# A two-layer sequence kernel on one core: the attention's numerator on GpSimd, and three reorderings of TensorE and VectorE work

## The reference

```python
x = L0_attn_hidden                                  # (2, 1024, 128)
x = layernorm(x + rwkv_attention(x))                # block 1: recurrence over time
x = layernorm(x + fp8_linear(x))                    # block 2
x = layernorm(x + conv_gate_long_convolution(x))    # block 3: by FFT in the reference
x = layernorm(x + routed_experts(x))                # block 4: 2 rounds, top 2 of 8 experts

# block 1, per time step (expo 0, 1 and 2 of the kernel are e1s, e2s and e2/e1):
out = (e1 * num + e2 * cv) / (e1 * den + e2)        # the attention's output
num, den = e1s * num + e2s * cv, e1s * den + e2s    # the state
rwkv = (sigmoid(r) * out) @ Wo

# block 4, twice:
shared_ctrl = gelu(ctx @ w_s1 + b_s1) @ w_s2 + b_s2
ctrl = gelu(ctx_e @ w1[expert] + b1) @ w2[expert] + b2
x_next, v_next = mix(inl(shared_ctrl, ...), inl(ctrl, ...))
halt = sigmoid(gelu(x_next @ w_h1 + b_h1) @ w_h2 + b_h2)
integrated += halt * (gelu(x_next @ w_f1 + b_f1) @ w_f2 + b_f2) * integration_weight
```

## Time and profile before

| | |
|---|---|
| median of 3 runs | 454.08 us (452.54 to 455.95) |
| the profiled execution's own time | 453.8 us |
| span of its instructions | 452.0 us |
| TensorE | 409.1 us busy, 91% of the span |
| VectorE | 337.3 us, 75% |
| ScalarE | 192.9 us, 43% |
| GpSimd | 21.8 us, 5% |
| the chain that ended last | TensorE 64%, VectorE 13%, ScalarE 3%, issue 2% |

### The profile page before, as it was taken

How to read it: one execution, slowest core, us unless ns; L and a number is a source line. 1 busy time by engine, 2 the same in 40 slices (tenths; PEclk the granted TensorE clock), 3 DMA queues, 4 the chain that set the end, 5 groups by cost and what they waited for, 6 DMA issues and landing times.

```text
span 452.0 us, 4385 instructions
## 1 busy us (share of the span) xinstructions
PE 409.1 (91%) x1494; PEld 215.4 (48%) x1494; DVE 337.3 (75%) x688; ACT 192.9 (43%) x318; POOL 21.8 (5%) x38
## 2 busy tenths in 40 slices
PE   4791987979999999999999889999999999999992
PEld 1341565667976375354544343433644433443361
DVE  5999998977882996879988994697654862374565
ACT  1342669452226513445255355344055626225431
POOL 1000203021000000000000000000000000000001
PEclk9896999879999999999999989999999999999997
DMA  6300000040000000000000000000000000000001
GB/s 227 133 1 0 1 1 0 2 151 0 1 1 0 1 1 0 0 1 1 1 1 0 0 1 23 0 1 1 0 0 1 24 1 0 1 0 0 0 1 46
DMA packets 4886, 7.10 MB, mean 16 GB/s; under 512 B 1031, under 2 KB 3713, under 8 KB 4737
## 3 DMA queue, kind: packets, MB, share of 16 engines
q1 hardware_dynamic: 3932, 4.78, 3.1%
q10 hardware_dynamic: 933, 2.04, 1.3%
HBM read 5.78 MB, written 1.05 MB: 15 GB/s over the span
## 4 chain that ended last, share of the span: by engine, by line
PE 64%; DVE 13%; ACT 3%; issue 2%; POOL 1%; POOLq 0%; DVEq 0%
PE ring L1291 21%; PE ring L1271 6%; PE ring L1286 4%; PE bankA L198 4%; PE ring L1273 3%; PE ring L1299 3%; PE ring L1306 2%; PE ring L1313 2%; PE ring L1310 2%; PE ring L1317 2%; PE timebank L300 2%; PE bankA L300 2%; PE specbank L275 2%; PE ring L1308 2%; PE ring L1314 1%
## 5 line engine op out<-in xcount | busy, mean ns | idle before, releaser
L1291 PE MATMUL ring<-hm,wc 128*128 128x512 f32 (+1 forms) x252 | 108.6, 581 | 0.0
L1291 PEld LDWEIGHTS ring<-hm,wc 128*128 128x128 f32 x252 | 46.2, 190 | 61.0 <-issue 53.0
L1500 DVE SCALAR_TENSOR_TENSOR hm<-xtm,cst,h 128x512 f32<-128x512 bf16 x48 | 33.2, 746 | 2.7 <-ACT h L1405 2.7
L198 PE MATMUL bankA<-wconv,h2w 128*128 128x256 f32 x128 | 35.0, 425 | 0.0
L1419 ACT ACTIVATE gts<-ring 128x512 f32<-128x512 f32 (+1 forms) x18 | 9.9, 550 | 49.0 <-PE ring L1291 49.0
L1405 ACT ACTIVATE h<-ring,vec 128x512 f32<-128x512 f32 x32 | 21.9, 686 | 17.7 <-PE ring L1273 15.2
L198 PEld LDWEIGHTS bankA<-wconv,h2w 128*128 128x128 f32 x128 | 26.0, 212 | 5.5 <-issue 2.0
L1589 DVE SCALAR_TENSOR_TENSOR f2e<-hl,f2e 128x512 f32<-128x512 f32 (+1 forms) x9 | 5.7, 631 | 26.1 <-ACT hl L1450 26.1
L1286 PE MATMUL ring<-hm,wc 64*128 64x512 f32 (+1 forms) x84 | 22.9, 621 | 1.2 <-DVE hm L1500 1.2
L1271 PE MATMUL ring<-zs,wc 128*128 128x512 f32 x40 | 20.9, 603 | 0.3 <-DVE zs L1591 0.3
L1416 ACT ACT_TABLE_LOAD x8 | 10.3, 1283 | 25.1 <-PE ring L1291 25.1
(11 more groups left out here) (274 smaller groups left out, 791.3 us busy)
## 6 DMA issues: line engine op xcount, KB each, us to landing
wc<-in_w_c SPq DMA_DIRECT2D x1, 1664.0 KB
out<-xall SPq DMA_DIRECT2D x8, 128.0 KB, 1.9
cst<-in_const ACTq DMA_DIRECT2D x1, 838.5 KB, 10.7
wc<-in_x_feat SPq DMA_DIRECT2D x1, 768.0 KB, 11.7
wc<-in_k_time ACTq DMA_DIRECT2D x1, 512.0 KB
bconv<-in_bcast SPq DMA_DIRECT2D x1, 512.0 KB, 10.7
wc<-in_x_feat ACTq DMA_DIRECT2D x1, 256.0 KB, 3.7
wa<-in_w_a SPq DMA_DIRECT2D x1, 256.0 KB, 3.8
```

The costliest lines, as they stand in the source:

```text
L198: ins = pe.matmul(at, h2w[:, n, u % 2, u // 2:u // 2 + P], wconv[:, tap, :], start=False, stop=(h == HALVES - 1 and tap == TAPS - 1))
L1291: ins = pe.matmul(dst[:, at], wc[:, w:w + P], hm[:, seat(j, made + g - 1), at], start=False, stop=(g == PAIRS - 1))
L1500: dve.scalar_tensor_tensor(hm[:, seat(j, k), :], picked, cst[:, C_EG + g:C_EG + g + 1], h[:, g, :], ALU.is_equal, ALU.mult).then_inc(S["hm ...
```

## The change

Four edits, all in the order of work or in who does it; the amount of arithmetic is unchanged.

1. The product and the sum that make the attention's numerator (L877, L879) leave VectorE. GpSimd does both on the same tiles, in its turn between the two norms' factors. It starts when the denominator is made (semaphore `denominator`), and waits for its own product before the sum. VectorE goes from the denominator to the reciprocal, and waits for `numerator` ahead of the last product, behind the rounding and L883.
2. `project` is parted into `project_key` and `project_value`. In turn 2 TensorE turns the normed chunk between the two. In turn 3 the turn stands ahead of the forward transform of the convolution's first half.
3. Third job: VectorE does only the spectra (L327, L328) ahead of `pick(2)`, and the ten products of the convolution's last chunk behind `post_last(2)`. TensorE has two of job 3's hidden tiles behind `h1` of job 2 and no longer ahead of the logits, and the forward transform of the last half behind `halt`.
4. At the end VectorE norms job 6's chunk ahead of both refinements of job 7, and makes both halves' statistics before both halves' norms.

```diff
@@ first stage, PE @@
-                def project(c):
+                def project_key(c):
...
+                def project_value(c):
...
@@ one(c) of first_pe @@
-                    project(c + 1)
-                    if c == CHUNKS - 1:
-                        pe.wait_ge(kv_copied, CHUNKS)
-                        pe.wait_ge(piece_kept, BATCH)
-                        forward_half(pe, 0, 0, pskv)
+                    if c < CHUNKS - 1:
+                        project_key(c + 1)
+                    if c < CHUNKS - 2:
+                        project_value(c + 1)
                     if c <= CHUNKS:
                         turn2(c - 2)
+                        if c == CHUNKS - 2:
+                            project_value(c + 1)
+                        if c == CHUNKS - 1:
+                            pe.wait_ge(kv_copied, CHUNKS)
+                            pe.wait_ge(piece_kept, BATCH)
+                            forward_half(pe, 0, 0, pskv)
                         piece(pe, c - 2, 0, 0)
                         turn1(c - 1)
@@ first_pool @@
+                def attended(c):
+
+                    pool.wait_ge(denominator, c + 1)
+                    after(pool, wo_done, c)
+                    pool.tensor_tensor(ta[:, :], expo[:, 2, :], vsb[:, :], ALU.mult).then_inc(numer_product, 1)
+                    pool.wait_ge(numer_product, c + 1)
+                    pool.tensor_tensor(pair(ta[:, :]), pair(ta[:, :]), prev(num, c), ALU.add).then_inc(numerator, 1)
+
                 def one(c):
                     if valid(c - 1):
                         pool.wait_ge(var1, c)
                         after(pool, x1_ready, c - 1)
                         factors(norms[0], rstd1)
+                    if valid(c):
+                        attended(c)
                     if valid(c - 1):
                         pool.wait_ge(var2, c)
@@ first_dve @@
                 def output(c):
                     dve.wait_ge(exp_out, c + 1)
                     dve.wait_ge(scans_done, 2 * BATCH * (c + 1))
-                    after(dve, wo_done, c)
-                    rec.go(dve.tensor_tensor(pair(dn[:, :]), pair(expo[:, 2, :]), prev(den, c), ALU.add))
-                    rec.link(dve.tensor_tensor(ta[:, :], expo[:, 2, :], vsb[:, :], ALU.mult))
+                    dve.tensor_tensor(pair(dn[:, :]), pair(expo[:, 2, :]), prev(den, c), ALU.add).then_inc(denominator, 1)
+                    dve.wait_ge(denominator, c + 1)
                     rec.go(dve.reciprocal(dn[:, :], dn[:, :]))
-                    rec.go(dve.tensor_tensor(pair(ta[:, :]), pair(ta[:, :]), prev(num, c), ALU.add))
 
                 def output_end(c):
                     rec.wait()
                     rec.link(dve.scalar_tensor_tensor(dn[:, :], thr[:, :], 1.0, dn[:, :], ALU.add, ALU.mult))
+                    dve.wait_ge(numerator, c + 1)
                     dve.tensor_tensor(rwkv[:, :], ta[:, :], dn[:, :], ALU.mult).then_inc(rwkv_ready, 1)
@@ order @@
                 turn_back(1)
-                hiddens(3, 2, HU)
+                hiddens(3, 2, 3)
                 logits(2)
                 pair(2, GATE)
                 spread(2)
-                tail_around(2, lambda: forward(3, 1))
-
+                tail(2, "f1a")
+                tail(2, "f1b")
+                tail(2, "h1")
+                hiddens(3, 3, HU)
+                tail(2, "f2")
+                tail(2, "halt")
+                forward(3, 1)
                 beta(3)
@@ block.vector @@
                 post_beta(2)
-                products(dve, 3, 0, Xb)
+                spectra(dve, 3, 0, Xb)
                 pick(2)
                 post_gate(2)
                 post_last(2)
+                products_now(dve, 3, 0, Xb, ready=True)
                 choices(2)
+                products_late(dve, 3, 0, Xb)
                 masks_early(3)
@@ end of block.vector @@
                 finish_stats(6)
+                finish_norm(6)
                 refine(7, 0)
-                finish_norm(6)
                 refine(7, 1)
                 finish_stats(7, 0)
+                finish_stats(7, 1)
                 finish_norm(7, 0)
-                finish_stats(7, 1)
                 finish_norm(7, 1)
```

More of the change, by code:

```diff
@@ L513, in two_layers @@
             scans_done = sem("scans_done")
+            denominator = sem("denominator")
+            numer_product = sem("numer_product")
+            numerator = sem("numerator")
             rwkv_ready = sem("rwkv_ready")
@@ L674, in first_pe @@
             def first_pe(pe):
[L675 to L687 removed]
+                def project_key(c):
+                    if c == 1:
+                        pe.wait_ge(a_in, 16)
+                    after(pe, k_copied, c)
+                    pe.matmul(psk[:, :], wmix[:, 0, 0, :], cur(hT, c), start=True, stop=False)
+                    pe.matmul(psk[:, :], wmix[:, 1, 0, :], prev(hT, c), start=False, stop=True).then_inc(k_done, 1)
+                def project_value(c):
+                    after(pe, kv_copied, c)
+                    for q, dst in ((1, psv), (2, psr)):
+                        pe.matmul(dst[:, :], wmix[:, 0, q, :], cur(hT, c), start=True, stop=False)
+                        ins = pe.matmul(dst[:, :], wmix[:, 1, q, :], prev(hT, c), start=False, stop=True)
+                    ins.then_inc(kvr_done, 1)
                 def turn2(c):
```

16 lines of the change are left out of this document (3 added, 13 removed).

## The result

The changed kernel takes 442.48 us (median of 4 runs, 441.70 to 444.41), beside 454.33 us for the kernel before on the same chip. The ratio is 0.9752, with a 95% interval of 0.9723 to 0.9782. The forecast was 444.6 us in a range of 440.5 to 449.5. The gain is 11 to 12 us where 9.2 were forecast. Three executions of all that follow took 466, 610 and 1057 us (of the kernel before, of the end alone and of TensorE's part of the third job) and count in no ratio.

What follows compares the result with a forecast made beforehand. VectorE was taken to bound the first stage (88% busy) and TensorE the rest (95%). First stage, third job and end sum: 453.8 - 3.6 - 3.7 - 1.9 = 444.6 us, range 440.5 to 449.5.

Steps and rivals of the forecast that it cites:

- The numerator on GpSimd: First stage: VectorE loses two steps per turn, GpSimd's work hides beside the reciprocal; gain 1.17 us turn 0, 1.15 turn 1.
- Turn 2: First stage: with keys and values parted, q comes at about 61.0 and the rounding follows the reciprocal; gain 1.2 us.
- Turn 3: First stage: TensorE idles, then turns ahead of the forward transform; gain between +1.2 and -0.4 us, 0.1 taken.
- the case worked out for a falling clock: Turn 3: idle 3 us lower TensorE's clock, the transform takes up to 1.7 us longer, q is some 1.0 us late.
- the first stage's 3.6 us: Sum of the gains in turns 0 to 3 of the first stage: 3.6 us, from 3.1 to 4.7.
- Rival E: More than forecast: turn 3 gains its 1.2 us and the clock stays up; 439.5 to 441 us, chance 0.08.
- The third job: Earlier pick and `xn`; job 4 starts at 276.6 instead of 280.25 after waiting about 1.1 us; gain 3.7 us.
- The end: Last norms: second refinement 0.4 us earlier, GpSimd's power overlaps the second half's statistics, 1.5 us; gain 1.9 us.
- Rival B: First stage: GpSimd's steps do not run beside the reciprocal and hold VectorE; 449 to 454 us, chance 0.12.
- rival D: First stage: GpSimd's steps outlast their cover, so `rwkv` is late every turn; slower than 458.3 us, chance 0.03.

Runs made afterwards that it cites:

- The first trace: Profiled execution of the changed kernel, all four edits, from its first measurement: 441.7 us, with a span of 439.6 us.
- the second measurement: The unaltered changed kernel measured again against the kernel before, with more rounds: 442.86 us, ratio 0.9745; its trace has a span of 441.7 us.

## Why the prediction was right, and where it was not

- **The numerator on GpSimd**: right in mechanism and size. 1.27 and 1.18 us a step against 1.2 taken, both inside the reciprocal, 1.15 us gained in turn 0 (1.17 forecast) and in turn 1 (1.15). The 1.2 us were chosen between 0.5 us and several without a near row, so the good fit is in part luck.
- **Turn 2** (1.2 forecast): the wait for q that edit 1 alone would meet was shown (1.15 us), and that edit 2 removes it. The first trace gives 3.23 - 2.01 = 1.22 us. The second gives 0.14, and the trace of edits 1 and 2 loses 0.15 us, for a reason that was no step of the sum. TensorE's low clock of turn 1 lasted longer in both, so the taps' spectra took 6.17 and 6.47 us instead of 5.10, and VectorE waited 0.94 and 1.24 us for L725.
- **Turn 3** (0.1 taken, bounds -0.4 to 1.2): the bounds hold, the value within them is not a fixed number. The gain is 1.20 us where the clock stayed up, 0.02 and about -0.1 us where it fell, behind an idle time that is 3.02 us in all three. The prediction named a wait of over 1 us for q in turn 3 as a sign that it is wrong. That sign is there in two of the three traces (1.09 and 1.25 us): the case worked out for a falling clock happened.
- **The step that was missing**: turn 4's low clock. The prediction carried the first stage's 3.6 us unchanged to the third job, and so put turn 4 at nothing. Before, TensorE ran at 0.50 for some 6 us behind two waits of 1.25 and 1.40 us; filling these gave 2.1 us (1.2 to 3.1) on the kernel before, and the change gets 2.2 to 2.3 us there for nothing. Rival E spoke of the clock staying up, but in turn 3 and not here. Its 439.5 to 441 us do not follow from its condition: 1.2 us in turn 3 in place of 0.1 make 443.5, and no term is given for the rest.
- **The third job** (3.7 forecast): 3.78 us in both traces. One step inside it was mis-sized: TensorE waits 0.42 us for `zs`, not 1.1, since it needs 17.3 us from `xn` to job 4 and not 16.7 (with edit 3 alone, from 259.46 to 277.20 less the wait). VectorE's side, which ends last, came as forecast, so the gain did too. The split shows that what pays first is VectorE's order; TensorE's alone gives nothing, since it only lengthens the wait for the pick to 4.61 us.
- **The end** (1.9 forecast): 1.9 us in the traces, 2.1 us alone.
- **The total** is in the range partly because errors cancel. In the second measurement's trace the steps of the sum gave 2.23 + 0.14 + 0.02 + 3.78 + 1.9 = 8.1 us of the 9.2 forecast, and turn 4's 2.2 us, which were not in it, made it 10.3.
- **Rival B** did not happen, and its mechanism is real. It missed only because both steps lie beside the one long VectorE instruction that does not hinder them. The cover worked out for rival D was wrong for the same reason: 4.1 and 7.0 us counted all VectorE work up to the last product as cover, and of that work only the reciprocal's 3.35 us were. Past that VectorE pays for the overlap, also in turns where nobody waits for the numerator.

What isn't settled: why the same waits are followed by a low clock in one order and one execution and not in another. The traces show that it is so, and what it costs.

## What to carry to other kernels

When work goes to GpSimd, look at what VectorE does meanwhile, not only at whether the result is in time: here 2.45 us beside a reciprocal cost nothing, and the same steps beside scans, or a longer product beside roundings, cost VectorE 1.5 to 2 us in most turns. Where two engines wait for each other, try each half of a reordering alone; here both halves were needed in the first stage (edit 2 without edit 1 gave nothing), and in the third job TensorE's half gained only together with VectorE's. And list every place where TensorE idles for one to three us and then runs at half clock, since a change ahead of it, or only the next execution, can make that stretch 1 to 2 us shorter or longer.

## What the runs showed of the hardware

- GpSimd makes a 128x512 product or sum of two f32 tiles in 1.27 or 1.18 us; VectorE takes 0.69. GpSimd's product took 1.77 us where it started behind a two-input VectorE instruction.
- A VectorE step that starts while such a GpSimd step is on ends 0.3 to 0.6 us behind it: a scan 1.69 us instead of 0.73, `scalar_tensor_tensor` 1.24 instead of 0.69, single-input `tensor_scalar` 1.28 instead of 0.43. The reciprocal stays at 3.35 us beside them.
- An idle time of 3.02 us on TensorE, at the same place of the same program, was followed by a granted clock of 1.00 in one execution and of 0.57 (mean of the window 72 to 75) in another. One of 1.40 us behind one of 1.25 was followed by 0.50 in the kernel before, and by 1.00 in the changed one. The low stretch behind these two waits lasted some 6 us in before and some 3 us in a kernel with the same first stage.
- Two extra 128x512 matmuls with an unread result, put into such waits, took 2.1 us off the whole.
